# A delta-rule scan on one core: the retrieval's matmuls stream 32 columns instead of 96

## What is computed

```
def step(S, inp):
    q_t, k_t, v_t, beta_t = inp
    retrieval = jnp.einsum('bhij,bhj->bhi', S, k_t)
    S = S + jnp.einsum('bhi,bhj->bhij', beta_t * (v_t - retrieval), k_t)
    o_t = jnp.einsum('bhij,bhj->bhi', S, q_t)
    return (S, o_t)
```

## Time and profile before

| | us |
|---|---|
| median of 3 runs | 1123.03 |
| lowest and highest run | 1112.12, 1125.03 |
| the profiled execution, its own time | 1123.51 |
| its span, first to last instruction | 1121.8 |
| TensorE matmuls busy | 933.7 |
| TensorE weight loads busy | 709.0 |
| VectorE busy | 926.6 |
| mean granted clock of TensorE | 0.911 |

### The profile page before, as it was taken

The page is one execution under the profiler, slowest core; times in us unless marked ns, Lnnn a source line. Parts: engine busy times, 40 slices in busy tenths (PEclk is TensorE's granted clock), DMA queues, the critical chain, the costliest instruction groups (busy, mean ns, idle before and its releaser), DMA issues.

```text
span 1121.8 us, 19571 instructions
## 1 busy us (share of the span) xinstructions
PE 933.7 (83%) x6107; PEld 709.0 (63%) x6114; DVE 926.6 (83%) x2750; ACT 663.2 (59%) x1603; POOL 434.6 (39%) x655
## 2 busy tenths in 40 slices
PE   7688999999999999999999989899797610696056
PEld 7466777877887878878788777666565410343044
DVE  4767699999999999999999997666665879799887
ACT  2467566766566666666666653546575532586097
POOL 4323345465364553644535443315366660000000
PEclk8789799999999999999999998899988955798589
DMA  9900000000300000000000000213200000000012
GB/s 139 139 1 6 5 7 10 6 9 9 117 11 6 7 10 6 10 7 6 11 6 9 8 5 11 84 58 127 99 1 0 1 0 0 1 1 1 0 62 89
DMA packets 30150, 30.49 MB, mean 27 GB/s; under 512 B 7137, under 2 KB 25441, under 8 KB 30049
## 3 DMA queue, kind: packets, MB, share of 16 engines
q1 hardware_dynamic: 28128, 29.12, 10.8%
q10 hardware_dynamic: 1920, 0.14, 0.2%
HBM read 20.85 MB, written 4.19 MB: 22 GB/s over the span
## 4 chain that ended last, share of the span: by engine, by line
PE 64%; DVE 23%; ACT 6%; issue 5%; DMA 1%; ACTq 1%; DVEq 0%
PE ps L1770 7%; PE ps L1778 7%; PE ps L1709 5%; PE psG L1732 5%; DVE work L1645 5%; PE psY L1746 4%; PE psX L1746 4%; PE ps L1890 4%; PE psY L1824 3%; PE psY L1911 3%; PE psX L1824 3%; PE psG L1726 3%; PE ps L1838 2%; PE psX L1911 2%; PE psG L1890 2%
## 5 line engine op out<-in xcount | busy, mean ns | idle before, releaser
L510 POOL TENSOR_TENSOR arena<-arena 128x256 f32<-128x256 f32 x32 | 23.3, 729 | 306.5 <-DVE arena L1078 303.3
L603 ACT ACTIVATE arena<-ps 128x512 f32<-128x512 f32 x128 | 72.9, 596 | 48.1 <-PE ps L1770 47.9
L1770 PE MATMUL ps<-work 32*128 32x256 f32 x512 | 93.5, 406 | 2.4 <-ACT work L649 2.3
L478 POOL TENSOR_SCALAR_AFFINE_SELECT arena<-arena 128x2048 f32<-128x2048 f32 x32 | 92.1, 2879 | 2.2
L568 ACT ACTIVATE arena<-ps,nparity 32x256 f32<-32x256 f32 x124 | 51.1, 458 | 49.4 <-PE ps L1709 49.0
L1732 PE MATMUL psG<-arena 128*128 128x512 f32 x128 | 73.6, 658 | 2.4 <-DVE arena L1144 2.4
L1770 PEld LDWEIGHTS ps<-work 32*128 32x128 f32 x512 | 61.9, 186 | 19.4 <-issue 12.9
L1709 PE MATMUL ps<-work,arena 128*128 128x64 f32 x496 | 63.8, 285 | 6.7 <-DVE work L1104 6.7
L1089 DVE TENSOR_TENSOR arena<-arena 128x256 f32<-128x256 f32 (+1 forms) x96 | 66.5, 692 | 3.3
L1092 DVE TENSOR_REDUCE arena<-arena 128x64 f32<-128x256 f32 (+1 forms) x96 | 65.9, 687 | 3.3
L1746 PEld LDWEIGHTS psY<-work,arena 128*128 128x128 f32 x512 | 60.4, 196 | 12.4 <-DVE arena L1161 10.7
(11 more groups left out here) (328 smaller groups left out, 2612.0 us busy)
## 6 DMA issues: line engine op xcount, KB each, us to landing
arena<-in_mask_BxSxS_ik SPq DMA_DIRECT2D x8, 1024.0 KB, 6.7
xs<-arena SPq DMA_DIRECT2D x256, 16.0 KB, 1.8
arena<-in_ctx SPq DMA_DIRECT2D x8, 512.0 KB, 4.1
out<-xs SPq DMA_DIRECT2D x32, 128.0 KB, 1.7
arena<-in_x SPq DMA_DIRECT2D x8, 384.0 KB, 24.0
arena<-in_L_ffn_w SPq DMA_DIRECT2D x2, 1024.0 KB, 24.2
arena<-in_L_attn_w_qkvb SPq DMA_DIRECT2D x2, 512.0 KB, 5.8
arena<-in_x SPq DMA_DIRECT2D x8, 96.0 KB, 7.7
```

The costliest lines, as they stand in the source:

```text
L478: G.affine_select(out=pairs, in_=pairs, compare_op=ALU.is_ge, fill=0.0, base=0, pattern=[[0, NH], [-CT, B], [0, CT]], channel_multiplier=1 ...
L603: A.activation(attn[j % 2][:, r * 512:(r + 1) * 512], ps[(2, 0)[r % 2]][:, :], ACT.Copy).then_inc(att_out, 1)
L1770: last = M.matmul(ps[(2, 0)[r % 2]][:, f * 2 * P:(f + 1) * 2 * P], kq[j % 4][rows, f * P:(f + 1) * P], qe[rows, f].rearrange("p e t -> p ( ...
```

## The change

The moving operand is head h's 32 columns alone, taken from `kq[m % 4]`, and the result goes to head h's columns alone. The weights, the number of products, the waits and the signal are the same. `padded` and the clearing of its zero rows stay.

```diff
-                first = 2 * (m % 4)
-                rows = padded[:, first:first + 3, :].rearrange("p z (k h t) -> p h z k t", k=2, t=CT)
+                rows = kq[m % 4].rearrange("p (k h t) -> p h k t", k=2, t=CT)
                 into = psR[m % 2][:, :].rearrange("p (h k t) -> p h k t", k=2, t=CT)
                 for h in range(NH):
-                    a, b = 1 if h == 0 else 0, 2 if h == NH - 1 else 3
-                    last = M.matmul(into[:, h - 1 + a:h - 1 + b], sexp[:, h, :], rows[:, h, a:b],
-                                    start=False, stop=True, skip_group_check=True)
+                    last = M.matmul(into[:, h], sexp[:, h, :], rows[:, h], start=False, stop=True, skip_group_check=True)
                 last.then_inc(ret_mm, 1)
```

## The result

The change makes the kernel slower. Its median is 1261.17 us (four runs, 1259.31 to 1264.81) against 1121.84 us before; the ratio is 1.1277, with a 95% interval from 1.1224 to 1.1329. The profiled execution took 1259.31 us, 135.8 more than that of before (1123.51). By the medians the change costs 139.3 us. The forecast was 1260 us, in a range from 1160 to 1345.

What follows compares the result with a forecast made beforehand. TensorE was taken to bound the scan, with VectorE within some tenths of a microsecond. Unchanged instructions cost 0; 287 us at low clock x 0.474 = 136 us, added to 1123.5, gave 1260 us, range 1160 to 1345.

Steps and rivals of the forecast that it cites:

- The pace of the retrieval: Retrieval on TensorE: weight loads, 0.112 us each, set the pace at 32 columns too; effect taken as 0.
- Rival B: Retrieval gets faster with fewer columns, VectorE's 0.34 us wait a step is all the gain: 1113 us; chance 3%.
- The clock: TensorE behind each retrieval: clock falls to 0.50 without idle time, returns after dense work; near 0.80 from 300 to 500 us.
- Rival A: Clock holds through the scan, the step stays at 20.21 us: 1123 us; chance 12%.
- How long: Low clock behind each retrieval: 6.83 + 3.42 = 10.25 us in a step.
- C: Short fall: grams behind the retrieval restore the clock after 3.42 us a step; 41 us lost, 1165 us; chance 14%.
- D: Long fall: clock returns only before the next state products; 8.35 us lost a steady period, 1340 us; chance 17%.
- The price: TensorE at low clock: work takes 1.90 times as long, so each microsecond there loses 0.474 us.
- The sum: Whole scan: 256 us at low level in 25 steady periods plus 31 elsewhere, 287 x 0.474 = 136 us.
- filled in: Periods at the scan's edges, already partly at low clock: raised to 10.25 us each, 31 us more at it.

Runs made afterwards that it cites:

- e1_64: Kernel before, with the retrieval streaming 64 columns, one zero row in place of two: 1119.73 us, ratio to before 1.0009.
- e3_added: The change, with a bf16 product of 256 columns of zeros ahead of each head's retrieval product: 1127.61 us, ratio to before 1.0069.
- e7_elsewhere: The change, with 8 products of 512 columns of zeros behind the values in passes 3 to 31: 1298.01 us, ratio to before 1.1571.
- e4_gram_first: The change, with each far gram moved ahead of its two attention groups: 1181.89 us, ratio 1.0552.

## Why the prediction was right, and where its terms were off

*The pace of the retrieval.* It was said to go by the weight loads. It does: 3.76 us with 96 and with 64 columns, 3.73 with 32. Rival B falls.

*The clock.* It was said to fall behind the retrieval in every step, with TensorE busy throughout, and to come back after the dense work. It does, and e1_64, e3_added and e7_elsewhere tie it to what streams there. Rival A falls: the clock fell in the change without any idle time, and the loads, as many in e1_64 as in the change, don't hold it. The evidence that the prediction had against A was thin: of its two stretches, the one at 116.90 lies just behind a wait of 3.11 us, so only the one in the last chunk began with a busy engine. The rule of the Trainium skill ("TensorE: Matmul & The Clock Gate", section "Loop structure matters more than you think"), that matmuls back to back stay warm, doesn't hold in this trace: TensorE was busy for 13.65 of 13.65 us at 0.50.

*How long.* This term was too small. The forecast took 10.25 us in every step; they are 10.24 and 13.65 by turns, 13 and 12 times in the 25 steady periods, together 297 us for 256. Neither C nor D came true in the change; e4_gram_first has a mixture, with no fall in some periods.

*The price.* This term was too large. The forecast took 0.474 us of loss for each microsecond at the low level. A pair of periods loses 24.88 + 26.32 - 2 x 20.21 = 10.78 us for 23.89 us at it, which is 0.451. The first half of attention takes 2.67 us for 1.73, only 1.54 times as long: its second group waits for a copy by ScalarE (L585, 0.45 us at either level). The forecast's ratio of 1.90 came from products that wait for no other engine.

*The sum.* Its 25 steady periods were to lose 256 x 0.474 = 121 us. By the lengths of those periods in the two kernels they lose 639.30 - 506.73 = 132.6 (0.446 for each of the 297 us):

```profile
148.82:655.55 506.73, 500.44 (x3750) 404.31 (x3751) 467.38 (x1205) 324.73 (x862) 252.72 (x384) 1.00 0.05 14
655.55:677.01 21.46, 18.50 (x121) 14.08 (x122) 18.34 (x47) 10.82 (x30) 10.99 (x16) 0.92 0.03 8
677.01:697.46 20.45, 18.19 (x119) 13.69 (x118) 16.97 (x42) 8.14 (x20) 5.56 (x3) 0.92 0.03 8
71.06:697.46 626.40, 606.04 (x4439) 487.91 (x4438) 561.29 (x1449) 394.35 (x1072) 297.35 (x444) 0.98 0.05 13
```

```profile
67.34:94.40 27.06, 25.25 (x151) 18.68 (x150) 18.51 (x47) 17.68 (x62) 9.37 (x13) 0.79 0.02 5
94.40:120.91 26.51, 25.06 (x151) 18.32 (x151) 18.57 (x50) 18.77 (x64) 9.91 (x15) 0.81 0.02 6
120.91:145.90 24.99, 24.75 (x150) 18.38 (x151) 21.45 (x66) 14.59 (x39) 9.94 (x15) 0.80 0.02 5
...
785.20:808.79 23.59, 22.82 (x121) 15.89 (x121) 18.45 (x48) 10.08 (x28) 9.90 (x15) 0.71 0.03 7
808.79:830.55 21.76, 21.00 (x119) 14.45 (x119) 17.05 (x43) 8.12 (x20) 5.57 (x3) 0.76 0.03 6
```

The first of these fences is the kernel before, the second the change, whose 25 steady periods lie between 145.90 and 785.20 us. The other periods were to lose 31 x 0.474 = 15 us and lost far less: the first three take 78.56 us for 77.76, the two at the end 45.35 for 41.91, and all that lies outside the first and the last retrieval is 1.0 us shorter (3.7 less ahead of the scan, where nothing was changed, and 2.7 more behind it). Together 132.6 + 0.8 + 3.4 - 1.0 = 135.8 us, against 136 forecast. So the time was met by a mechanism that was right and three terms that were off and made up for each other: 16% more time at the low level than forecast in the steady periods, at a price 6% lower, and 12 us less at the edges. There the second period, for which nothing was filled in, became 2.05 us shorter, and the first, the third and the last two lost less than was filled in. That the two totals agree within 1 us is luck: by the medians the loss is 139.3 us, and the runs of the kernel before alone lie up to 13 us apart.

Not tried was whether the content of the streamed columns matters; all fillers here are zeros. Each column that streams also writes a column of PSUM, so the runs don't show which of the two counts.

## What to carry to other kernels

Before work is taken off TensorE, look whether it sets the pace there at all: behind fp32 loads of 128 weight columns, 32 moving columns take as long as 96, and the columns that look like waste may be what holds the clock. Read the granted clock stretch by stretch, since TensorE's busy share is the same (99%) at 1.00 and at 0.76; and where thin work must be, put dense work beside it, or products of zeros into it, and try both.

## What the runs showed beyond what was expected

A bf16 product of 256 columns, put between fp32 products, cost 0.03 us (0.48/16) and not the 0.11 expected; the load of the fp32 weights behind it begins with it and runs beside it (both at 413.61 us in e3_added). And the low stretches of the change came in two lengths by turns, 10.24 and 13.65 us, for the whole steady part, so a model with one length for every step can have the right mean at best.
